# Attention scores of two groups at once in four PSUM banks, with 64-row matmuls for the low part of g, maxima read from PSUM and three output banks in turn

## The chip, the cores and the metric

The kernel runs on one core of one Trainium2 chip. The metric is the time of one execution on the device, in microseconds (us). A core has a matrix engine (TensorE, PE in the profile; its weight loads are PEld), VectorE (DVE), ScalarE (ACT), GpSimd (POOL) and SyncE (SP), whose queue issues the transfers here. They run side by side and wait for one another by semaphores. Matmul results land in PSUM, eight banks of 128 partitions x 512 f32; all else is in SBUF.

## The reference

A group norm, then self-attention over the 4096 pixels of each of four images of 256 channels, then two residual additions:

```python
x: (4, 256, 64, 64) float32;  C = 256, CQ = 64, N = 4096
xg = group_norm(x, G=32, eps=1e-5)           # per image
xf = xg.reshape(4, 256, 4096)
f = Wq @ xf;  g = Wk @ xf;  h = Wv @ xf      # 64, 64 and 256 rows
scores = f.T @ g                             # n x m, 4096 x 4096
beta = softmax(scores, axis=n)               # over n, for each column m
out = x + gamma * (h @ beta) + xf
```

## The kernel before, in words

Each f32 operand of a matmul is split into an f16 high and an f16 low part. The products kept are high x high, high x low and low x high.

An image (a batch) is cut into 16 column blocks of M = 256 columns m; there are K = 64 blocks. The 4096 rows n of a block are 32 tiles of 128, in G = 8 groups of GT = 4 tiles. A group of scores is thus 4 tiles x 256 columns, 1024 f32 on each partition, two banks.

`scores(q)` (L346, matmuls L354 and L355) computes group q = 8k + g into `S`. The stationary operand is a tile of `F1`, with the high part of f on partitions 0 to 63 and its low part on 64 to 127. `G1` holds the high part of g on both halves, `GL` the low part on both halves. Two matmuls of 128 rows and 256 columns per tile give (fh + fl) x (gh + gl). ScalarE's `store` (L451) copies `S` into `SC` in SBUF. VectorE's `maximum` (L586, the first a copy L579, the last into `MX` by L584) folds `SC` into the running maximum `XM`, in PSUM, in halves of 512 columns. `quadrant_maxima` (L591, L593, L600), a tiny f32 matmul `share_maxima` (L376), `column_maxima` (L608) and `spread_maxima` (L615) turn this into a row `MB` of column maxima. `subtract` (L621) takes it off the stored scores, `exps` (L457, L458) on ScalarE makes the exponentials, once rounded to f16 (`PH`) and once f32, and GpSimd's `low_weights` (L277) makes the low part `PL`. `weigh(n)` (L368 to L370) multiplies a group by V, 24 matmuls of 256 or 257 columns (the extra column of ones gives the softmax's denominator), accumulating in two banks of `O`, the pair of banks `k % 2`. `divide` (L640) and `scale_output` (L647) then finish the block, `turn_blocks` (L655) turns it in 32 x 32 blocks, 16 small transfers regroup these (`regroup` on SP), and GpSimd adds the residual.

The order of each engine is written out by hand. The main loop goes over n = 8k + g. TensorE computes the scores of group n + 16, two blocks ahead, and then weighs group n. VectorE subtracts for group n + 4, ScalarE makes the exponentials of n + 3, GpSimd the low weights of n + 3. The rings of `PH` and `PL` have 4 places, so exponentials of n + 3 wait until group n - 1 is weighed. SP, once per block, regroups and stores the block before and loads the residual input of the next.

Work for the next image is mixed in: in blocks j = 1 to 4 of an image (at g = 5) statistics, in block 5 the variances (`group_variances`, L529 to L544), in block 6 the roots (`inverse_roots`, L550 to L564), in blocks 7 to 10 normalising (L568) and splitting of x. In blocks 13 and 14 stand the f/g projections, `project_fg` (eight units of 512 columns, 6 matmuls each, L329 to L331; the evacuation is `round_fg` L463 to L465 and `low_fg` L627 to L629), in block 15 and block 0 of the next image the V projections, `project_v` (eight units of 4 tiles, 24 matmuls each, L341 to L343; `round_v` L471, `low_v` L635). They use the pair of `O` banks of the other parity. Before the loop, a head does all this for the first image, and the scores of blocks 0 and 1.

PSUM: `O` four banks, `S` two, `XM` one, `MB` one.

## Time and profile before

| what | us |
|---|---|
| median of 3 runs | 2033.85 (2032.63 to 2034.09) |
| the profiled execution | 2034.04 |
| its span, first to last instruction | 2032.3 |
| TensorE busy, matmuls | 1954.7 |
| VectorE busy | 1712.7 |
| ScalarE busy | 1611.6 |
| GpSimd busy | 1313.2 |

The span runs from the first to the last instruction; the time of an execution has a little more around it. Busy times of matmuls are modelled from their starts, and a matmul's duration is longer than the distance to the next one's start, since they are pipelined; so starts are to be compared, not durations. A row of the timeline gives the start, the duration, the engine, the line, the operation and its operands, and in brackets how long the engine was idle before it and who released it.

### The profile page before, as it was taken

The numbers are of one execution on the slowest core, as the hardware profiler recorded it, in microseconds if no ns is written. First come the engines' busy times: TensorE is split into PE (matmuls) and PEld (weight loads), VectorE is DVE, ScalarE is ACT, GpSimd is POOL, SyncE is SP. The second block draws the span as 40 slices with busy tenths as digits, with TensorE's granted clock in tenths as the row PEclk, the third lists the DMA queues.
The fourth block names the chain that finished last, engine by engine and source line by source line (L and its number), as shares of the span: only waits on it lengthen the run. The fifth ranks groups of instructions, "written<-read, shape, count | busy, mean of one in ns | idle before, by whom it ended". The sixth has DMA issues, their size and how long they took to land.

```text
span 2032.3 us, 43482 instructions
## 1 busy us (share of the span) xinstructions
PE 1954.7 (96%) x17476; PEld 1698.7 (84%) x17476; DVE 1712.7 (84%) x2469; ACT 1611.6 (79%) x1699; POOL 1313.2 (65%) x746
## 2 busy tenths in 40 slices
PE   3899999999999999999999999999999999999999
PEld 1688888888788888888778888888878888888887
DVE  8798899988868899998886989999787778887784
ACT  4588878888767887988876888788887788888885
POOL 3066668886546666887544676688645566667667
PEclk9899999999999999999999999999999999999999
DMA  2012211211002221221110221121111011111111
GB/s 96 1 32 72 71 31 43 73 30 30 19 20 69 55 62 27 66 61 22 27 22 23 67 71 51 22 73 51 30 22 27 17 32 22 32 30 30 32 22 43
DMA packets 188746, 82.68 MB, mean 41 GB/s; under 512 B 148352, under 2 KB 181376, under 8 KB 188544
## 3 DMA queue, kind: packets, MB, share of 16 engines
q1 hardware_dynamic: 188544, 79.90, 14.8%
q8 instruction: 137, 2.24, 0.5%
q14 instruction: 65, 0.53, 0.1%
HBM read 46.53 MB, written 16.78 MB: 31 GB/s over the span
## 4 chain that ended last, share of the span: by engine, by line
PE 87%; DVE 9%; issue 2%; ACT 1%; DMA 1%; SPq 0%; DVEq 0%; ACTq 0%
PE O L369 20%; PE O L370 20%; PE O L368 20%; PE S L354 10%; PE S L355 10%; DVE XM L586 2%; DVE SC L621 2%; PE O L341 1%; PE O L343 1%; PE O L342 1%; PE O L329 1%; PE O L331 1%; PE O L330 1%; DMA SC<-x 1%; DVE gt L556 1%
## 5 line engine op out<-in xcount | busy, mean ns | idle before, releaser
L277 POOL TENSOR_TENSOR PL<-SC,PH 128x1024 f16<-128x1024 f32 x512 | 1091.9, 2135 | 683.9 <-ACT SC L458 679.6
L369 PE MATMUL O<-V,PH 128*128 128x256 f16 x4096 | 1119.9, 273 | 0.0
L368 PE MATMUL O<-V,PH 128*128 128x257 f16 x4096 | 1116.4, 273 | 2.0 <-DVE GL L629 2.0
L370 PE MATMUL O<-V,PL 128*128 128x257 f16 x4096 | 1113.4, 272 | 0.0
L451 ACT ACTIVATE SC<-S 128x1024 f32<-128x1024 f32 x512 | 524.3, 1024 | 275.4 <-PE S L355 273.1
L586 DVE TENSOR_TENSOR XM<-SC,XM 128x512 f32<-128x512 f32 x896 | 616.2, 688 | 134.2 <-ACT SC L451 119.6
L621 DVE TENSOR_TENSOR SC<-SC,MB 128x1024 f32<-128x1024 f32 x512 | 618.8, 1209 | 0.7
L457 ACT ACTIVATE PH<-SC 128x1024 f16<-128x1024 f32 x512 | 537.6, 1050 | 27.5 <-DVE SC L621 19.4
L458 ACT ACTIVATE SC<-SC 128x1024 f32<-128x1024 f32 x512 | 536.1, 1047 | 0.0
L354 PE MATMUL S<-G,F 128*128 128x256 f16 x2048 | 479.0, 274 | 18.2 <-ACT SC L451 13.6
L355 PE MATMUL S<-GL,F 128*128 128x256 f16 x2048 | 479.1, 274 | 0.0
L370 PEld LDWEIGHTS O<-V,PL 128*128 128x128 f16 x4096 | 402.4, 98 | 52.6
L368 PEld LDWEIGHTS O<-V,PH 128*128 128x128 f16 x4096 | 394.3, 96 | 61.3 <-issue 2.8
L369 PEld LDWEIGHTS O<-V,PH 128*128 128x128 f16 x4096 | 396.1, 97 | 56.5 <-issue 0.3
L354 PEld LDWEIGHTS S<-G,F 128*128 128x128 f16 x2048 | 206.4, 101 | 47.5 <-ACT SC L451 11.2
L355 PEld LDWEIGHTS S<-GL,F 128*128 128x128 f16 x2048 | 201.3, 98 | 23.9 <-issue 0.3
L635 DVE TENSOR_TENSOR V<-O,V 128x1024 f16<-128x1024 f32 x32 | 39.2, 1225 | 78.4 <-ACT V L471 78.4
L296 POOL TENSOR_TENSOR RES<-RES,ATT 128x512 f32<-128x512 f32 x63 | 81.8, 1299 | 1.5 <-DMA ATT<-OT 1.5
L471 ACT CAST V<-O 128x1024 f16<-128x1024 f32 x32 | 32.4, 1012 | 60.6 <-PE O L343 60.6
L341 PE MATMUL O<-wvh,XH 128*128 128x256 f16 x256 | 70.6, 276 | 9.9 <-issue 6.8
L286 POOL TENSOR_SCALAR RES<-xres,rscale,rbias 128x256 f32<-128x256 f32 x128 | 78.7, 624 | 0.0
L342 PE MATMUL O<-wvl,XH 128*128 128x256 f16 x256 | 70.5, 275 | 0.0
(81 smaller groups left out, 1000.8 us busy)
## 6 DMA issues: line engine op xcount, KB each, us to landing
xin<-x SPq DMA_DIRECT2D x24, 1024.0 KB, 5.7
xres<-x SPq DMA_DIRECT2D x64, 256.0 KB, 2.9
out<-RES SPq DMA_DIRECT2D x64, 256.0 KB, 2.2
ATT<-OT SPq DMA_DIRECT2D x1008, 16.0 KB, 1.9
SC<-x SPq DMA_DIRECT2D x4, 1024.0 KB, 8.4
wv<-wvT SPq DMA_DIRECT2D x1, 256.0 KB, 10.3
wqk<-wqT SPq DMA_DIRECT2D x1, 64.0 KB, 10.5
wqk<-wkT SPq DMA_DIRECT2D x1, 64.0 KB, 10.5
```

The source lines that it names most:

```text
L277: pool.tensor_tensor(PL[:, s % RING, :], sc(s), PH[:, s % RING, :], ALU.subtract).then_inc(pl_ready, 1)
L341: mm(o, xh, wvh[:, h, :], start=h == 0, stop=False)
L354: mm(S[:, i * M:(i + 1) * M], f, G1[:, cols], start=True, stop=False)
L355: m = mm(S[:, i * M:(i + 1) * M], f, GL[:, cols], start=False, stop=True)
L368: mm(o[:, 0:C + 1], PH[:, n % RING, cols], vh, start=t == 0, stop=False)
L369: mm(o[:, 0:C], PH[:, n % RING, cols], vl, start=False, stop=False)
L370: w = mm(o[:, 0:C + 1], PL[:, n % RING, cols], vh, start=False, stop=t == T - 1)
L451: nc.scalar.activation(sc(q), S[:, :], ACT.Copy).then_inc(s_stored, 1)
L457: nc.scalar.activation(PH[:, s % RING, :], sc(s), ACT.Exp, bias=SHIFT)
L458: nc.scalar.activation(sc(s), sc(s), ACT.Exp, bias=SHIFT).then_inc(exp_done, 1)
L586: ve.tensor_tensor(XM[:, :], part, XM[:, :], ALU.max).then_inc(s_maxed, 1)
L621: ve.tensor_tensor(tile, tile, MB[:, 0:M].unsqueeze(1).to_broadcast([P, GT, M]), ALU.subtract).then_inc(sub_ready, 1)
```

## The change

**Scores.** `S` has four banks, two for an even group and two for the odd one after it. `scores(q)` runs at even g only and computes groups q and q + 1. For each group the high part of g is multiplied as before, by matmuls of 128 rows (4 per group). The low part is multiplied by the high part of f alone, in matmuls of 64 rows: `F1` now has the high part of f on partitions 0 to 63 for even units of 512 columns and on 64 to 127 for odd ones, so that of a pair of groups one uses the upper and the other the lower half of the array. Order: four full, eight half (alternating between the groups), four full.

**Maxima.** VectorE takes a group's maximum straight from `S` in one operation of 1024 columns, with `XM` now in SBUF. The first group of a block has none of its own: the second is compared with the stored copy of the first. VectorE takes the odd group while ScalarE stores the even one, then they change places. Once per block `fold_maxima` reduces 1024 to 256 columns. TensorE waits for both maxima and both stores before the next scores.

**Output banks.** `O` has three banks: block k uses banks 2k and 2k + 1 modulo 3, the third (`spare`) serves the shared maxima and the projections. `weigh` runs by bank, 12 matmuls for the first and 12 for the second. V projections are units of two tiles, 16 per image, in the middle (`MID`) or at the end (`END`) of a group.

**Doubling g.** ScalarE and VectorE write g's parts once; a transfer per unit on SP (`double_g`) copies both parts to the other half. The weights Wq are loaded a second time, so that odd units come out of the projection with the halves changed. Weights and V have another place or stride.

The core of the diff:

```diff
+        GG = sb("GG", [P, 2, N], f16)
+        G1, GL = GG[:, 0, :], GG[:, 1, :]
+        XM = sb("XM", [P, GW], f32)
-        O = ctx.enter_context(nc.psum_tensor("O", [P, 2, MB2, 512], f32))
-        S = ctx.enter_context(nc.psum_tensor("S", [P, GW], f32))
-        XM = ctx.enter_context(nc.psum_tensor("XM", [P, 512], f32))
+        O = ctx.enter_context(nc.psum_tensor("O", [P, OB, 512], f32))
+        S = ctx.enter_context(nc.psum_tensor("S", [P, 2, GW], f32))
...
+            def double_g(u):
+                f, g = halves(u)
+                n = slice(u % NFG * FGW, (u % NFG + 1) * FGW)
+                sp.wait_ge(fg_done, u + 1)
+                sp.dma_start(GG[f, :, n], GG[g, :, n]).then_inc(g_in[u % NFG], 16)
...
             def scores(q):
-                if q > 0:
-                    pe.wait_ge(s_stored, q)
-                for i in range(GT):
-                    f = F1[:, (g * GT + i) * P:(g * GT + i + 1) * P]
-                    mm(S[:, i * M:(i + 1) * M], f, G1[:, cols], start=True, stop=False)
-                    m = mm(S[:, i * M:(i + 1) * M], f, GL[:, cols], start=False, stop=True)
-                m.then_inc(s_ready, 1)
+                for a in range(2):
+                    if q > 0:
+                        pe.wait_ge(s_maxed, q)
+                        pe.wait_ge(s_stored, q - 1 + a)
+                    for i in (0, 2):
+                        mm(to(a, i), F1[:, rows(a, i)], G1[:, cols], start=True, stop=False)
+                for i in (0, 2, 1, 3):
+                    for a, half in enumerate((slice(0, CQ), slice(CQ, P))):
+                        mm(to(a, i), F1[half, rows(a, i)], GL[half, cols], start=i % 2 == 1, stop=i % 2 == 0)
+                for a in range(2):
+                    for i in (1, 3):
+                        m = mm(to(a, i), F1[:, rows(a, i)], G1[:, cols], start=False, stop=True)
+                    m.then_inc(s_ready, 1)
...
+                if g % 2 == 0 and k + 2 < K:
...
                     scores(n + 2 * G)
+                pe.wait_ge(pl_ready, n + 1)
...
+                weigh(n, 0)
+                extra(k, g, MID)
+                if g == 2 and k + 1 < K:
...
+                    share_maxima(k + 1, spare(k))
+                if g == 0 and k > 0:
+                    pe.wait_ge(osb_ready, MB2 * (k - 1) + 1)
+                weigh(n, 1)
+                extra(k, g, END)
...
             def store(q):
                 act.wait_ge(s_ready, q + 1)
+                if q % 2 == 1:
+                    act.wait_ge(s_maxed, q)
...
+            for s in range(EXP_LEAD):
+                exps(s)
             for n in range(K * G):
                 if n + EXP_LEAD < K * G:
                     exps(n + EXP_LEAD)
+                if g % 2 == 0 and k + 2 < K:
+                    store(n + 2 * G)
+                    store(n + 2 * G + 1)
...
+            def fold_maxima(c):
+                dve.wait_ge(s_maxed, G * (c + 1))
...
+                ve.tensor_reduce(MX[:, :], XM[:, :].rearrange("p (i m) -> p m i", i=GT), axis=AX.X,
+                                 op=ALU.max).then_inc(mx_ready, 1)
+            def maximum(q):
+                c, g = divmod(q, G)
+                scores = S[:, q % 2, :]
+                dve.wait_ge(s_ready, q + 1)
+                if g == 0:
+                    return
+                if g == 1:
+                    dve.wait_ge(s_stored, q)
...
+                    ve.tensor_tensor(XM[:, :], scores, sc(q - 1), ALU.max).then_inc(s_maxed, 2)
+                    return
+                if q % 2 == 0:
+                    dve.wait_ge(s_stored, q + 1)
+                dve.wait_ge(s_maxed, q + 1 if q % 2 == 0 else q - 1)
+                ve.tensor_tensor(XM[:, :], scores, XM[:, :], ALU.max).then_inc(s_maxed, 1)
...
+            for s in range(SUB_LEAD):
+                subtract(s)
             for n in range(K * G):
                 if g == 0 and k > 0:
                     divide(k - 1)
+                    scale_output(k - 1)
+                if g % 2 == 0 and k + 2 < K:
+                    maximum(n + 2 * G + 1)
                 if n + SUB_LEAD < K * G:
                     subtract(n + SUB_LEAD)
+                if g % 2 == 0 and k + 2 < K:
+                    maximum(n + 2 * G)
+                if g == 7 and k + 2 < K:
+                    fold_maxima(k + 2)
```

## Rows read from the trace of the kernel before

**Rows 1.** The page: busy time by engine, and the granted clock by slice (tenths).

```profile
PE 1954.7 (96%) x17476; PEld 1698.7 (84%) x17476; DVE 1712.7 (84%) x2469; ACT 1611.6 (79%) x1699; POOL 1313.2 (65%) x746
...
PEclk9899999999999999999999999999999999999999
```

**Rows 2.** The page: the chain that ended last, by engine.

```profile
PE 87%; DVE 9%; issue 2%; ACT 1%; DMA 1%; SPq 0%; DVEq 0%; ACTq 0%
```

**Rows 3.** Timeline of VectorE, the reciprocals: start us, us, engine, line, operation, idle before.

```profile
242.55 0.17 DVE L640 RECIPROCAL rden<-O 128x2 f32<-128x2 f32 x1 [0.89 <-PE O L370]
...
360.07 0.16 DVE L640 RECIPROCAL rden<-O 128x2 f32<-128x2 f32 x1
...
473.02 0.17 DVE L640 RECIPROCAL rden<-O 128x2 f32<-128x2 f32 x1 [0.89 <-PE O L370]
...
626.27 0.17 DVE L640 RECIPROCAL rden<-O 128x2 f32<-128x2 f32 x1 [0.76 <-PE O L370]
...
1701.59 0.17 DVE L640 RECIPROCAL rden<-O 128x2 f32<-128x2 f32 x1 [0.89 <-PE O L370]
...
1729.88 0.17 DVE L640 RECIPROCAL rden<-O 128x2 f32<-128x2 f32 x1 [0.89 <-PE O L370]
```

**Rows 4.** Timeline of TensorE, last V matmuls, scores, first weighing (98 to 101.3 us).

```profile
98.05 0.27 PE L341 MATMUL O<-wvh,XH 128*128 128x256 f16 x1
...
100.34 0.27 PE L354 MATMUL S<-G,F 128*128 128x256 f16 x1
...
101.21 0.27 PE L368 MATMUL O<-V,PH 128*128 128x257 f16 x1
```

**Rows 5.** Timeline of ScalarE in a plain block (1727 us).

```profile
1727.23 1.03 ACT L451 ACTIVATE SC<-S 128x1024 f32<-128x1024 f32 x1 [0.60 <-PE S L355]
1728.15 1.05 ACT L457 ACTIVATE PH<-SC 128x1024 f16<-128x1024 f32 x1
```

**Rows 6.** The waits: who waited for whom, us, times, longest.

```profile
ACT SC L451 <- PE S L355: 273.1, 420, 2.1
```

**Rows 7.** Timeline of VectorE in a plain block (1705 us).

```profile
1705.08 1.21 DVE L621 TENSOR_TENSOR SC<-SC,MB 128x1024 f32<-128x1024 f32 x1
1706.21 0.69 DVE L586 TENSOR_TENSOR XM<-SC,XM 128x512 f32<-128x512 f32 x1
1706.81 0.70 DVE L591 STREAM_TRANSPOSE MT<-MX 128x512 f32<-128x512 f32 x1
```

**Rows 8.** Timeline of TensorE's loads and matmuls after a wait (1007.4 us).

```profile
1007.40 0.10 PEld L368 LDWEIGHTS O<-V,PH 128*128 128x128 f16 x1 [0.92 <-issue]
1007.44 0.27 PE L368 MATMUL O<-V,PH 128*128 128x257 f16 x1 [0.67 <-DVE GL L629]
```

**Rows 9.** Timeline of TensorE around the f32 matmuls of the maxima (1711.9 us).

```profile
1711.94 0.31 PE L376 MATMUL O<-mxs,alike 128*128 128x32 f32 x2
1712.08 0.27 PE L354 MATMUL S<-G,F 128*128 128x256 f16 x1
```

**Rows 10.** Groups of instructions by line and form: busy us, mean ns, idle before.

```profile
L635 DVE TENSOR_TENSOR V<-O,V 128x1024 f16<-128x1024 f32 x32 | 39.2, 1225 | 78.4 <-ACT V L471 78.4
...
L471 ACT CAST V<-O 128x1024 f16<-128x1024 f32 x32 | 32.4, 1012 | 60.6 <-PE O L343 60.6
...
L376 PEld LDWEIGHTS O<-mxs,alike 128*128 128x128 f32 x128 | 19.3, 191 | 5.7 <-DVE mxs L600 5.0
```

**Rows 11.** Timeline of VectorE: variances, roots and the maximum after each, a normalising.

```profile
261.03 0.60 DVE L529 BATCH_NORM_AGGREGATE mv<-stats 128x2 f32<-128x48 f32 x2
...
269.86 0.70 DVE L586 TENSOR_TENSOR XM<-SC,XM 128x512 f32<-128x512 f32 x1
...
293.29 0.22 DVE L550 TENSOR_SCALAR gt<-gvar 128x4 int32<-128x4 int32 x1
...
300.98 0.69 DVE L586 TENSOR_TENSOR XM<-SC,XM 128x512 f32<-128x512 f32 x1
...
324.40 3.35 DVE L568 TENSOR_SCALAR xin<-xin,nmean,nrstd 128x1024 f32<-128x1024 f32 x2
```

More of the change, by code:

```diff
@@ L142, in groupnorm_attention @@
         fg_done = sem("fg_done")
+        g_in = [sem(f"g_in{i}") for i in range(NFG)]
         v_ready = sem("v_ready")
@@ L252, in _ @@
                         load(b + 1, p)
+                    for place, i in FG_AT.items():
+                        if place[0] == j:
+                            double_g((b + 1) * NFG + i)
             store(K - 1)
```

378 lines of the change are left out of this document (198 added, 180 removed).

## Prediction, made before the changed kernel ran

> **What bounds the kernel now.** I read the page first. TensorE is busy 96% of the span, at the full clock in nearly every slice [rows 1], and 87% of the chain that ended last lies on it [rows 2]. So the time is nearly the sum of what TensorE issues. Next I took the timeline and looked for the period of the loop: the reciprocal L640 runs once per column block, so two of them in a row bound a block. A plain block takes 1729.88 - 1701.59 = 28.29 us [rows 3]. On TensorE, 21 matmuls of 256 columns start between 98.05 and 100.34, so one start follows the other after 0.109 us [rows 4]; I call this a slot. A duration of 0.27 us is the way of one matmul through the array, not its price. A block has 8 groups of 24 weighing and 8 score matmuls, 256 slots, and 256 x 0.109 = 27.9 us, so a plain block is TensorE without holes. In it ScalarE waits 0.60 us for TensorE's scores in each group of 28.29/8 = 3.54 us, so it works at most 2.94 us of it [rows 5]; over the run that wait is 273 us [rows 6]. VectorE spends 1.13 us on a subtraction and 0.60 us on half a maximum [rows 7].
>
> Where is TensorE not the limit? In blocks 5 to 8 of a batch, where VectorE has the group-norm arithmetic of the next batch to do: 360.07 - 242.55 = 117.52 us against 4 x 28.29 = 113.2, a loss of 4.4 us. And in blocks 13 to 15 and the next block 0, where the projections of the next batch are mixed in: 626.27 - 473.02 = 153.25 us against 113.2 + 20.9 for 192 V matmuls of a slot each + 10.5 for 48 f/g matmuls of 512 columns, two slots each: 8.7 us lost [rows 3]. Each happens three times.
>
> The profiled execution took 2034.04 us, its span 2032.3. The 1.7 us outside it stay. The median is 2033.85, so no correction is needed between the two.
>
> **The score matmuls (the gain).** Two groups cost 16 slots now, 1.744 us. After, they are 8 full matmuls and 8 of 64 rows. Two of the latter sit in different halves of the array and write different banks; if they run side by side, four slots hold the eight, and a pair costs 12 x 0.109 = 1.308 us. The main loop computes the scores of 62 blocks, 248 pairs, so each 0.1 us on a pair is 24.8 us. The full gain is 0.436 x 248 = 108.1 us.
>
> The trace of before has no matmul of 64 rows, so two prices are unknown. The first is the change between full and half array, twice a pair. Below, I take nothing: the f32 matmuls of L376 stand between f16 ones without a hole. Above, I take that the array must run empty first: 0.27 - 0.11 = 0.16 us of way left after a slot, and 0.04 us from a load to its matmul where TensorE came out of a wait (1007.40 and 1007.44), 0.20 us in all [rows 4, 8]. It cannot be below nothing, since no matmul is saved by it. The nearest row is L376: its two matmuls of 32 columns take 1712.08 - 1711.94 = 0.14 us, 0.07 each with its weight load, where 32 of 256 columns would be a few hundredths [rows 9]. Some 0.05 us over the columns is what an unlike matmul costs there, and I take 0.05 us per change, 0.10 per pair.
>
> The second is the rate of loads. Each half matmul has a load of its own; side by side, a load and a matmul must start every 0.055 us. The densest that the trace shows is again 0.07 us, for f32 weights, whose load takes 0.19 us against 0.10 for f16 [rows 8, 10]. I take 0.055 as reached, since an f16 load is half as long, and 0.07 as the other end.
>
> So a pair costs 1.308 + 0.10 = 1.408 us, and 0.336 x 248 = **83.3 us** go.
>
> The Trainium skill, "TensorEngine Tiling (Array Packing)", section Tiling Modes, Key Properties, says that changing the tiling mode drains TensorE, which speaks against this change. It gives no duration. By the row's bound the drains would take nearly the whole gain, and the time is the one of the third rival below.
>
> **The maxima and who waits for them.** Before, VectorE reads scores from SBUF after ScalarE stored them; TensorE waits for ScalarE only (`s_stored`). After, VectorE reads PSUM itself, and TensorE's next pair waits for both maxima (`s_maxed`). Behind that wait stands everything of TensorE. Load: before, a block has 8 subtractions and 16 half maxima, 8 x 1.13 + 16 x 0.60 = 18.6 us; after, 8 subtractions, 7 maxima and one fold, each of 1024 columns. The subtraction L621 also has one operand in PSUM and 1024 columns, so I price all at 1.13: 16 x 1.13 = 18.1 us, and the transpose and reduction after the fold halve to 256 columns [rows 7]. VectorE is not busier, but the block shrinks by 4 x 0.336 = 1.3 us.
>
> Does the handshake fit? Let a pair start on TensorE at 0; it lasts 48 x 0.109 + 1.41 = 6.6 us. Scores are ready at 1.5. VectorE: odd maximum to 2.6, subtraction to 3.8, even maximum to 4.9. ScalarE: two exponentials of at most 1.05 us from 0.2 to 2.3, even store (0.92) to 3.2, odd store to 4.1 [rows 5]. The next pair needs both at 6.6. At a block's start the divide and scale delay the odd maximum by about 1 us, but that pair has no even one. Cost in plain blocks: nothing; the cover is 1.7 us. ScalarE's work on a pair is at most 5.9 us, 0.7 less than the period, so it does not become the bound either.
>
> It does not fit where VectorE has a long uninterruptible run in group 5. Computing the variances takes 269.86 - 261.03 = 8.83 us and the roots 300.98 - 293.29 = 7.69 us [rows 11]. From the start of the pair of group 4: even maximum done 4.9, subtraction 6.05, variances 14.9, then odd maximum, subtraction, even maximum 18.3. TensorE wants to start the next block's scores at 13.3, so it stands 5.0 us; for the roots 3.9 us. Together 8.9 us per batch against the 4.4 lost now, so 4.5 x 3 = **13.5 us** are given back. Normalising (3.35 us in block 7, where 6.05 + 3.35 + 3.4 = 12.8) is just covered.
>
> **Projections, queues, head.** An f/g unit has two roundings and two low parts, not three; the third goes to a DMA on SP's queue, which waits there for `fg_done` behind the block's regroup and store and ahead of the next block's. Those are due later than the projections, and the doubled g is read a block or more later: nothing. But one spare bank now serves all projections, so each unit waits for the one before to be emptied; the order leaves some 1.3 us of weighing between two V units, and emptying 512 columns (a rounding, then a low part) takes about as long: half of 1012 and of 1225 ns, 1.1 us, and the signals [rows 10]. I book no difference to the 8.7 us lost per batch now, with 4 us per batch either way. The number of V and projection matmuls is the same. Splitting `weigh` by bank changes the order alone; the wait of its second half for `osb_ready` comes 2.6 us into a block, VectorE's scale is done at about 1.9: nothing. The new stride of V changes no count: nothing.
>
> In the head, f/g work on VectorE and ScalarE shrinks by a third, but the first subtractions and exponentials are no longer mixed into the V units: after the last V unit come rounding, low part, subtraction, two exponentials and the low weights, some 6 us, with only 1.4 us of scores over them. Now weighing begins at 101.21, right behind the scores [rows 4]. I take 3 us more, between -8 and +8.
>
> **The sum.** 2034.0 - 83.3 + 13.5 + 3 = 1967.2, so 1967 us.
>
> **The rivals.** *Free changes.* Changing array mode costs nothing: 2034 - 108.1 + 16.5 = 1942 us; were the VectorE stalls hidden too, 1926. For it: TensorE takes unlike matmuls without a hole. Against: L376's 0.07 us. *Loads set the half phase.* Eight halves at 0.07 us are 0.56, not 0.436 us: a pair costs 1.532, 0.212 x 248 = 52.6 us gained, 2034 - 52.6 + 16.5 = 1998 us. *Slower than before: the array empties at each change.* 0.40 us per pair, all but 0.036 x 248 = 8.9 us of the gain gone, while the new VectorE stalls and the head still cost 16.5: 2034 - 8.9 + 16.5 = 2042 us. The change turns slower when the two switches cost over 0.436 - 16.5/248 = 0.37 us a pair, 0.19 each. For it: no row shows matmuls of both array modes in flight together; against: none shows any emptying either. *The change does not do what it says:* the halves run one after the other, a slot each: 1.744 + 0.10 us a pair, 2034 + 24.8 + 16.5 = 2075 us. For it: each of them needs its own load.
>
> **How the numbers follow.** Forecast as summed, 0.45; free changes 0.23; loads 0.13; emptying 0.14; one after the other 0.05. The forecast's own range is 1950 to 1990. The range 1934 to 2043 cuts off the part of free changes with hidden stalls (0.08) and the upper half of the slow cases (0.11). A measurement of this kernel tells about 0.2% from no change, 4 us. Faster: the first three cases and a rest of the emptying, 0.82. Within 0.2%: 0.03, all from emptying that costs about 0.19 us a change. Slower: 0.15.
>
> **What would show it.** In the timeline of TensorE: half matmuls that start in pairs close together and four pairs in 0.44 us; the hole at the two changes, 0.05 us forecast; a plain block of 28.29 - 1.34 = 26.9 us between reciprocals. In the waits: TensorE's scores waiting for VectorE's maximum some 4 to 5 us in blocks 5 and 6 of each batch, and hardly elsewhere. ScalarE's wait for scores should fall to well under half of 273 us. The prediction is wrong if plain blocks have waits of TensorE on maxima (the handshake is tighter than worked out), if a maximum from PSUM costs clearly over 1.13 us, or if the pair of scores lies outside 1.31 to 1.71 us.

## The result, and the profile after

| what | before | after |
|---|---|---|
| median of 4 runs each, us | 2033.91 | 2014.78 (2013.05 to 2015.34) |
| span of the profiled execution, us | 2032.3 | 2013.6 |
| TensorE busy, matmuls, us | 1954.7 | 1915.7 |
| VectorE busy, us | 1712.7 | 1661.2 |
| ScalarE busy, us | 1611.6 | 1591.8 |

The changed kernel takes 0.9908 of the time of before (95% interval 0.9896 to 0.9921): 19 us faster, where 67 were forecast. Each ratio here and below is taken against executions of the kernel before in the same series (medians from 2032.35 to 2033.91), and each difference in us is against 2014.78 unless said. The lines of its page that answer [rows 1]:

```profile
PE 1915.7 (95%) x17476; PEld 1567.4 (78%) x17476; DVE 1661.2 (83%) x2021; ACT 1591.8 (79%) x1699; POOL 1312.0 (65%) x746
PEclk9899999999999998999999999999999999999999
```

I read the plain block first, against [rows 3]: the timeline of VectorE after, the reciprocals (now L741).

```profile
1693.08 0.23 DVE L741 RECIPROCAL rden<-O 128x1 f32<-128x1 f32 x2
...
1720.39 0.24 DVE L741 RECIPROCAL rden<-O 128x1 f32<-128x1 f32 x2
...
1747.69 0.22 DVE L741 RECIPROCAL rden<-O 128x1 f32<-128x1 f32 x2
```

A plain block takes 27.30 us, 0.99 less than the 28.29 of before, where 1.34 were forecast. Times 62 that is 61 us. Now the pair of scores in such a block, in the timeline of TensorE after (a row with x4 or x8 is so many instructions in a row, from the first start to the last end):

```profile
1732.77 0.60 PE L400 MATMUL S<-GG,F 128*128 128x256 f16 x4
1733.31 0.61 PE L403 MATMUL S<-GG,F 64*128 64x256 f16 x8
1733.85 0.61 PE L406 MATMUL S<-GG,F 128*128 128x256 f16 x4
1734.30 0.27 PE L418 MATMUL O<-V,PH 128*128 128x257 f16 x1
```

The pair lasts 1734.30 - 1732.77 = 1.53 us. Eight half matmuls end 0.61 us after the first starts; in single slots they would need 7 x 0.109 + 0.27 = 1.03. So they run two at a time, eight in the time of four. The view of stretches, for this line alone, gives the number under way (PE, in the first brackets) in two stretches of 0.02 us:

```profile
1733.38:1733.40 0.02, 0.02 (x2) 0.02 (x4) 1.00 0.00 0
1733.42:1733.44 0.02, 0.02 (x4) 0.01 (x2) 1.00 0.00 0
```

They come in pairs, one pair after the other at the distance of a slot. From the first of them to the next full matmul pass 0.54 us, four slots and 0.10; from the first full one to the first half, again 0.54, four slots and 0.10. So each change of the array's mode costs about 0.10 us, where 0.05 was taken. The first half matmul starts at 1733.31, while the four full ones end at 1732.77 + 0.60 = 1733.37: by these modelled ends the array is not empty at the change.

Then the blocks with the next image's arithmetic. Blocks 5 to 10 of the first image take 31.68, 32.81, 29.53, 28.07, 28.05 and 28.06 us, 14.4 us over six plain blocks; before, 4.4 were lost there. The two stalls of TensorE in its timeline after:

```profile
273.93 0.60 PE L400 MATMUL S<-GG,F 128*128 128x256 f16 x4 [2.85 <-issue]
...
306.69 1.04 PE L400 MATMUL S<-GG,F 128*128 128x256 f16 x4 [3.67 <-DVE XM L677]
```

Four matmuls behind the second stall take 1.04 us instead of 0.60. The view of stretches shows why; the third column from the end is the granted clock. After, from the first stall on:

```profile
273.90:276.75 2.85, 2.82 (x21) 1.87 (x22) 2.85 (x2) 2.59 (x3) 1.94 (x1) 0.69 0.01 3
276.75:303.00 26.25, 26.25 (x239) 21.85 (x237) 23.00 (x36) 18.77 (x20) 17.39 (x11) 0.97 0.14 31
306.69:309.56 2.87, 2.87 (x17) 1.55 (x18) 2.87 (x2) 2.61 (x3) 1.94 (x1) 0.50 0.00 0
309.56:316.00 6.44, 6.44 (x47) 5.17 (x46) 6.23 (x12) 4.18 (x5) 2.40 (x3) 0.77 0.01 3
316.00:339.00 23.00, 23.00 (x221) 19.15 (x219) 19.33 (x18) 19.62 (x21) 18.88 (x11) 1.00 0.16 35
```

and before, block 5 with the variances and block 6 with the roots:

```profile
242.55:275.52 32.97, 32.61 (x298) 28.63 (x297) 31.28 (x47) 25.51 (x28) 21.09 (x12) 1.00 0.18 54
275.52:306.64 31.12, 28.74 (x260) 24.95 (x259) 30.03 (x51) 23.35 (x26) 19.38 (x12) 1.00 0.11 27
```

After each of the two stalls TensorE works for a few us at its lower level of 1.2 GHz (0.50 right behind the second); before, it stays at the full clock in these two blocks. The part of the clock that is missing is worth 0.31 x 2.85 + 0.03 x 26.25 + 0.50 x 2.87 + 0.23 x 6.44 = 4.6 us per batch. Not all of that would come back at the full clock, as the kernel with the halves in a row shows below.

In blocks 8 to 10 nothing of that kind is left, yet each takes 0.76 us more than a plain block. The timeline of VectorE after, around the normalising in block 8:

```profile
385.52 3.35 DVE L650 TENSOR_SCALAR xin<-xin,nmean,nrstd 128x1024 f32<-128x1024 f32 x2
388.79 1.21 DVE L677 TENSOR_TENSOR XM<-S,XM 128x1024 f32<-128x1024 f32 x1
389.92 1.21 DVE L713 TENSOR_TENSOR SC<-SC,MB 128x1024 f32<-128x1024 f32 x1
391.05 1.21 DVE L677 TENSOR_TENSOR XM<-S,XM 128x1024 f32<-128x1024 f32 x1
392.18 1.21 DVE L713 TENSOR_TENSOR SC<-SC,MB 128x1024 f32<-128x1024 f32 x1
393.31 1.98 DVE L656 TENSOR_REDUCE MX<-XM 128x256 f32<-128x1024 f32 x1
395.21 0.21 DVE L741 RECIPROCAL rden<-O 128x1 f32<-128x1 f32 x2
395.46 1.00 DVE L749 TENSOR_SCALAR OSB<-O,rden,gam 128x256 f32<-128x256 f32 x2
```

and what TensorE then waits for:

```profile
396.06 0.28 PE L418 MATMUL O<-V,PH 128*128 128x257 f16 x1 [0.21 <-DVE OSB L749]
```

VectorE comes out of the 3.35 us with no pause up to the reciprocal, so `divide` and `scale_output` of the block before are late, and TensorE waits for the bank that they empty. Start to start, this costs 0.38 us over a slot, half of the 0.76. The rest stands further on in the block, in the pair of scores and at `share_maxima`:

```profile
400.02 0.72 PE L400 MATMUL S<-GG,F 128*128 128x256 f16 x4
403.15 0.38 PE L427 MATMUL O<-mxs,alike 128*128 128x32 f32 x2
```

The second group's full matmuls come 0.13 us late, behind ScalarE's store, which ends at 400.22; `share_maxima` costs some 0.25 us more than in a plain block, behind VectorE's `mxs`, which ends at 403.01. The fold of the maxima is in VectorE's row of work too, and it takes 1.98 us where 1.13 were priced.

Head: the first reciprocal is at 135.76 instead of 129.41. The first weighing in the timeline of TensorE after, against the last row of [rows 4]:

```profile
106.29 0.40 PE L418 MATMUL O<-V,PH 128*128 128x257 f16 x1 [5.25 <-POOL PL L312]
```

It waits 5.25 us for the first low weights, starts 5.1 us later than before, and behind that wait, from 106.29 to 109.40, the granted clock is 0.50. Blocks 13 to 15 and the next block 0 take 150.07 us against 109.2 for four plain ones and 31.4 for the matmuls of the projections: 9.5 us lost per batch; before, 8.7 in the first batch and 7.0 in the other two. That difference of 1.6 us before is the clock too: TensorE stands 2.28 us in block 14 of the first batch and 2.29 in that of the second, but only behind the first, in the 6 us from 523.70, is the granted clock 0.72; behind the second it is 1.00. So the 8.7 us that the prediction took for each of three batches hold for one.

So from the reciprocals of all 64 blocks the difference comes together: 6.35 us at the first reciprocal, -60.1 for 61 blocks of scores behind it at 0.985, +29.5 for blocks 5 to 10 of three batches, +5.8 for the projections, -0.4 for the last two blocks, which compute no scores: -18.9. The last reciprocal is at 2008.14 instead of 2026.91, 18.8 earlier.

The waits after, of ScalarE and of TensorE for the maximum (us in total, times, longest), against [rows 6]:

```profile
ACT SC L524 <- issue: 133.2, 82, 5.2
ACT PH L530 <- PE O L420: 119.3, 233, 0.8
...
ACT SC L524 <- PE S L406: 7.4, 7, 2.9
...
PE S L400 <- DVE XM L677: 14.8, 5, 3.7
```

ScalarE's wait for scores is 7 us by name, but it has moved rather than gone: 133 us stand before the store with another cause, 119 before the exponentials, for a free place in the ring of `PH`.

### The profile page after: what moved, and what is told of

Same layout as the page of the kernel before. It is cut to its first block and busy times, and to the rows that moved or that the text cites. A ratio compares the mean times of both kernels' runs of the same rounds, so it can differ in the third digit from the quotient of the medians.

```text
span 2013.6 us, 44173 instructions
## 1 busy us (share of the span) xinstructions
PE 1915.7 (95%) x17476; PEld 1567.4 (78%) x17476; DVE 1661.2 (83%) x2021; ACT 1591.8 (79%) x1699; POOL 1312.0 (65%) x746
## 3 DMA queue, kind: packets, MB, share of 16 engines
q8 instruction: 139, 2.28, 0.5%
## 5 line engine op out<-in xcount | busy, mean ns | idle before, releaser
L524 ACT ACTIVATE SC<-S 128x1024 f32<-128x1024 f32 x512 | 502.6, 1013 | 150.4 <-issue 133.2
L677 DVE TENSOR_TENSOR XM<-S,XM 128x1024 f32<-128x1024 f32 x384 | 468.2, 1219 | 151.6 <-PE S L406 149.7
L400 PE MATMUL S<-GG,F 128*128 128x256 f16 x1024 | 157.6, 275 | 26.5 <-DVE XM L677 14.8
L406 PE MATMUL S<-GG,F 128*128 128x256 f16 x1024 | 160.2, 280 | 0.0
L403 PE MATMUL S<-GG,F 64*128 64x256 f16 x2048 | 159.6, 276 | 0.0
L400 PEld LDWEIGHTS S<-GG,F 128*128 128x128 f16 x1024 | 99.1, 98 | 47.7 <-issue 20.6
L406 PEld LDWEIGHTS S<-GG,F 128*128 128x128 f16 x1024 | 80.3, 99 | 62.5 <-issue 55.6
L403 PEld LDWEIGHTS S<-GG,F 64*128 64x128 f16 x2048 | 80.0, 95 | 61.6 <-issue 54.9
L656 DVE TENSOR_REDUCE MX<-XM 128x256 f32<-128x1024 f32 x64 | 125.6, 1962 | 0.1
L672 DVE TENSOR_TENSOR XM<-S,SC 128x1024 f32<-128x1024 f32 x64 | 78.4, 1225 | 53.8 <-ACT SC L524 52.6
L727 DVE TENSOR_TENSOR V<-O,V 128x512 f16<-128x512 f32 x64 | 43.7, 689 | 73.3 <-ACT V L544 73.3
L544 ACT CAST V<-O 128x512 f16<-128x512 f32 x64 | 37.1, 587 | 76.1 <-PE O L379 76.1
```

The costliest lines, as they stand in the source:

```text
L400: mm(to(a, i), F1[:, rows(a, i)], G1[:, cols], start=True, stop=False)
L403: mm(to(a, i), F1[half, rows(a, i)], GL[half, cols], start=i % 2 == 1, stop=i % 2 == 0)
L406: m = mm(to(a, i), F1[:, rows(a, i)], G1[:, cols], start=False, stop=True)
L524: nc.scalar.activation(sc(q), S[:, q % 2, :], ACT.Copy).then_inc(s_stored, 1)
L677: ve.tensor_tensor(XM[:, :], scores, XM[:, :], ALU.max).then_inc(s_maxed, 1)
```

## The experiments

Three things had to be told apart: what the scores' part is worth and what a change of mode costs; what the next image's arithmetic costs and by which mechanism; and whether the rest (head, fold, normalising) is what it seems. All diffs are against the changed kernel unless said.

**The low part of g on the full array.**

```diff
-    mm(to(a, i), F1[half, rows(a, i)], GL[half, cols], start=i % 2 == 1, stop=i % 2 == 0)
+    mm(to(a, i), F1[:, rows(a, i)], GL[:, cols], start=i % 2 == 1, stop=i % 2 == 0)
```

> The changed kernel, with the low part of g multiplied on the whole array (128 rows) as before, all else kept: no change of array mode, 16 slots per pair. Theory A, side by side works and each change of mode costs 0.10 us: a pair costs 1.744 us where the changed kernel's trace has 1.53, so a plain block takes 4 x 0.21 = 0.86 us more than 27.30, 28.15, and the run 248 x 0.21 = 53 us more, less what the longer blocks give VectorE back: 2055 to 2068 us, slower than the kernel before; the rest of the change then costs 20 to 35 us by itself. Rival B, the matmuls of 64 rows bring little and the gain comes from the maxima and the three banks: within 10 us of 2015.

Measured 2054.39 us, 1.0108 of before (1.0093 to 1.0123), 0.6 us under the range expected. Plain blocks take 28.20 us, 0.90 more than after, 0.225 a pair (0.436 for four slots less two changes: 0.105 each). So the 64-row matmuls are worth 40 us, and everything else in the change costs 22 us against before (2032.47 in this series).

**Four changes of mode instead of two.** Two full matmuls stand before and two behind the part shown.

```diff
+                for i in (0, 1):
+                    for a, half in enumerate((slice(0, CQ), slice(CQ, P))):
+                        mm(to(a, i), F1[half, rows(a, i)], GL[half, cols], start=i % 2 == 1, stop=i % 2 == 0)
+                for a in range(2):
+                    mm(to(a, 1), F1[:, rows(a, 1)], G1[:, cols], start=False, stop=True)
+                    mm(to(a, 2), F1[:, rows(a, 2)], G1[:, cols], start=True, stop=False)
+                for i in (2, 3):
+                    for a, half in enumerate((slice(0, CQ), slice(CQ, P))):
+                        mm(to(a, i), F1[half, rows(a, i)], GL[half, cols], start=i % 2 == 1, stop=i % 2 == 0)
```

> The changed kernel with its score matmuls in another order: two full, four half, four full, four half, two full, so four changes of array mode per pair for two, the same matmuls. Theory A, a change costs 0.10 us wherever it stands: 0.21 us more per pair, plain block 27.30 + 0.84 = 28.1, run 2014.8 + 50 = 2065 us. Rival B, the 0.2 us of holes in a pair are the pace of the half matmuls' loads or a price of the phase as a whole: nothing or less than 10 us more.

Measured 2055.19 us (1.0111, 1.0096 to 1.0126), 10 us under the expectation. Plain blocks take 28.14 us, 0.84 more, so 0.21 a pair and 0.105 us for each added change. Between the last start before and the first after a change the timeline has 0.09 to 0.10 us beyond a slot. The total rose by 40 and not by 62 x 0.84 = 52 us, since the blocks that wait for VectorE absorb a part (blocks 5 to 10 of the first image take 178.96 us here and 178.20 in the changed kernel). The two experiments give the same price by opposite routes: one takes two changes away, the other adds two. The Trainium skill, "TensorEngine Tiling (Array Packing)", Key Properties, says that a change drains TensorE. The trace agrees that a change costs time, but the 0.105 us is half of the 0.20 that [rows 4, 8] set as the price of an array that must run empty, and the half matmuls start before the modelled end of the full ones.

**The halves in a row.** All four halves of the upper group, then all four of the lower.

```diff
-    for i in (0, 2, 1, 3):
-        for a, half in enumerate((slice(0, CQ), slice(CQ, P))):
+    for a, half in enumerate((slice(0, CQ), slice(CQ, P))):
+        for i in (0, 2, 1, 3):
```

> The changed kernel with the eight 64-row matmuls in another order: the four of the upper half of the array, then the four of the lower, not alternating. Theory A, matmuls start in the order of the program and only neighbours in different halves run together: each but one takes a slot of its own, 3 x 0.109 to 4 x 0.109 us more per pair, a plain block 27.3 + 1.3 to 1.74 = 28.6 to 29.0 us, run 2014.8 + 80 to 105 = 2095 to 2120 us. Rival B, TensorE pulls the lower half's matmuls ahead: within 10 us of 2015.

Measured 2013.70 us (0.9904, 0.9891 to 0.9918), as after. The timeline of TensorE in this kernel:

```profile
1737.31 0.60 PE L400 MATMUL S<-GG,F 128*128 128x256 f16 x4
1737.85 0.62 PE L403 MATMUL S<-GG,F 64*128 64x256 f16 x8
1738.40 0.61 PE L406 MATMUL S<-GG,F 128*128 128x256 f16 x4
```

Eight halves again end in 0.62 us, and again two at a time. The first four in the program use one half of the array only, so if two run together because they sit in different halves, the lower four run beside upper ones that stand ahead of them in the program. My expectation that the order matters fell. Which half a record belongs to the trace does not tell, and a rival is left: a 64-row matmul might take half a slot wherever it sits. No run had all eight in one half. The Trainium skill, "TensorE: Matmul & The Clock Gate", Part 3 (what overlaps and what doesn't), has matmuls start strictly in program order; by that rule, with the slots of these rows, the lower four would start behind three slots of the upper, and I estimate 6 x 0.109 + 0.27 = 0.92 us for the eight. This run, with 0.62, speaks against it for matmuls in different rows of the array, unless the rival holds.

This kernel also shows what the lower clock is worth. In each of its three batches TensorE stands 3.67 us in block 6, and the granted clock behind it differs (third column from the end):

```profile
305.83:312.70 6.87, 6.87 (x42) 4.65 (x43) 6.74 (x9) 4.78 (x5) 4.27 (x2) 0.61 0.01 2
797.86:804.73 6.87, 6.87 (x50) 5.16 (x51) 6.74 (x9) 5.05 (x6) 4.26 (x2) 0.75 0.01 2
1289.13:1296.00 6.87, 6.15 (x57) 4.92 (x58) 6.76 (x9) 5.05 (x6) 4.28 (x2) 1.00 0.00 0
```

Block 7 takes 29.33, 28.51 and 27.72 us in them. So a stall of that length need not be followed by the lower clock, and the lowest of these clocks costs 1.6 us against the full one, though 0.39 x 6.87 = 2.7 us of clock are missing: at the full clock TensorE soon waits 0.72 us (at 1292.88) for VectorE's late scale.

**No variances and roots of the next image**, in the changed kernel and in the kernel before.

```diff
-                        group_variances(b + 1)
+                        pass
...
-                        inverse_roots(b + 1)
+                        ve.tensor_scalar(rscale[:, (b + 1) % 2, :], nrstd[:, 0:H], 1.0, None, ALU.add)
+                        ve.scalar_tensor_tensor(rbias[:, (b + 1) % 2, :], nmean[:, 0:H], -1.0, nrstd[:, 0:H],
+                                                ALU.mult, ALU.mult).then_inc(res_coefs, 1)
```

> The changed kernel without the variances and roots of images 1 to 3: they are normalised with the coefficients of image 0. Theory A, VectorE's long runs in blocks 5 and 6 hold back the maxima, so the scores, and the pause then lowers TensorE's clock, 9 to 10 us of stalls and slow matmuls net per image in blocks 5 to 7: 2015 - 25 to 30 = 1985 to 1990 us, with granted clock 1.00 in those blocks. Rival B, TensorE's lost time there is due to normalising and transfers: less than 8 us gained.

> The kernel before with the same part left out, the variances and roots of images 1 to 3. There a block 5 to 8 of an image loses 4.4 us in all and TensorE waits for ScalarE's stores alone. Theory A: 3 x 4.4 = 13 us gained, 2021 us, half of what the same edit gives the changed kernel, so the rest is the new wait and the clock. Rival B, the runs cost both kernels the same: the same 25 to 30 us, 2006 us.

Measured 1981.26 us (0.9745, 0.9729 to 0.9761), 33.5 less than after, 11.2 per batch and more than the 25 to 30 expected; and 2018.96 us (0.9933, 0.9918 to 0.9948), 13.5 less than before (2032.47 in this series), 4.5 per batch. In the first, blocks 5 and 6 take 27.26 and 27.24 us, in the timeline of VectorE:

```profile
244.73 0.23 DVE L741 RECIPROCAL rden<-O 128x1 f32<-128x1 f32 x2
...
271.99 0.23 DVE L741 RECIPROCAL rden<-O 128x1 f32<-128x1 f32 x2
...
299.23 0.22 DVE L741 RECIPROCAL rden<-O 128x1 f32<-128x1 f32 x2
```

and blocks 7 to 10 take 28.34 and three times 28.06: 3.3 us over plain blocks, which is the normalising alone. So the 14.4 lost per batch are 11.2 for this arithmetic (2.85 + 3.67 = 6.5 of stalls and 4.7 behind them, where the stretches gave 4.6 for the missing clock) and 3.3 for the normalising. Before, the whole loss of 4.4 was this arithmetic, and normalising was all but free (block 7 keeps 0.2 us).

**The same arithmetic in pieces.** First ten pieces, one at each of the groups 2 to 6 of blocks 5 and 6; then twelve smaller ones, the last two in groups 2 and 3 of block 7. A piece has one to five small operations; in the second kernel the steps of the roots' iteration come two at a time. The diff is that of the first.

```diff
-                    if j == VARS_AT:
...
-                        group_variances(b + 1)
-                    if j == ROOTS_AT:
-                        inverse_roots(b + 1)
...
+                if 2 <= g <= 6 and b + 1 < BATCH and j in (VARS_AT, ROOTS_AT):
+                    some_coefs(g, variance_steps if j == VARS_AT else root_steps, b + 1)
```

> The changed kernel with the same arithmetic for the variances and roots, cut into five pieces per block that stand at groups 2 to 6 of blocks 5 and 6 instead of one run at group 5. Theory A, it is the length of the run that holds back the maxima and then the clock: most of the 33.5 us that leaving the work out gave come back, 20 to 30 us, 1985 to 1995 us, blocks 5 and 6 at 28 us and clock 1.00 throughout. Rival B, VectorE has too much to do in these blocks whatever its order: under 12 us gained.

Measured 1998.34 us (0.9830, 0.9815 to 0.9844), 16.4 less: short of the expectation. TensorE still stalls for 2.06 us in block 6 (3.01 in the second batch). The cause is in the timeline of VectorE in this kernel, three operations on 4 numbers per partition:

```profile
293.03 1.50 DVE L642 SCALAR_TENSOR_TENSOR gt<-gr 128x4 f32<-128x4 f32 x1
294.56 1.20 DVE L643 TENSOR_TENSOR gt<-gt,gvar 128x4 f32<-128x4 f32 x1
295.79 2.05 DVE L644 SCALAR_TENSOR_TENSOR gr<-gt,gr 128x4 f32<-128x4 f32 x1
```

and of GpSimd:

```profile
292.38 2.13 POOL L312 TENSOR_TENSOR PL<-SC,PH 128x1024 f16<-128x1024 f32 x1 [1.20 <-ACT SC L531]
294.47 1.27 POOL L331 TENSOR_TENSOR RES<-RES,ATT 128x512 f32<-128x512 f32 x1
295.70 2.12 POOL L312 TENSOR_TENSOR PL<-SC,PH 128x1024 f16<-128x1024 f32 x1
```

Each of the three ends within 0.03 us of a GpSimd instruction (294.53 and 294.51, 295.76 and 295.74, 297.84 and 297.82); with GpSimd idle (from 291.2 to 292.4) the same operations take 0.16 us. The Trainium skill, "SBUF — State Buffer", Who interferes with whom, says that a VectorE instruction with two inputs in SBUF, or a copy or scalar operation in a two-port mode, and a GpSimd instruction that reads SBUF keep each other out for a whole instruction. The trace agrees, and it is why 8.83 and 7.69 us of [rows 11] are so long for so little data: before, L541 on 32 numbers per partition takes 2.12 us and ends at 266.33, beside low weights of GpSimd that end at 266.28.

> The changed kernel with the arithmetic of the coefficients in twelve pieces of at most two or three operations, at groups 2 to 6 of blocks 5 and 6 and groups 2 and 3 of block 7. In the run with ten pieces one piece of three operations took 4.75 us, as each waited for GpSimd, and TensorE stood 2.06 us behind it and then had a clock of 0.94. Theory A, only the length of the longest run counts: no stall over 1 us, clock 1.00, another 5 to 8 us gained on the ten pieces' 1998.3: 1990 to 1994 us. Rival B, the sum of VectorE's work in these blocks is the bound by now: within 3 us of 1998.

Measured 1989.93 us (0.9788, 0.9774 to 0.9801), 24.9 less, as expected. The stretches of blocks 5 to 7 in this kernel:

```profile
243.27:270.90 27.63, 27.63 (x264) 23.28 (x262) 26.53 (x39) 23.72 (x25) 19.65 (x12) 1.00 0.16 42
270.90:299.66 28.76, 28.53 (x270) 23.78 (x267) 27.84 (x40) 23.69 (x25) 19.39 (x12) 1.00 0.12 29
299.66:328.90 29.24, 27.48 (x258) 22.82 (x258) 28.82 (x35) 23.82 (x26) 21.16 (x12) 1.00 0.12 28
```

The clock stays full, with no stall over 1.10 us left. In the kernel with ten pieces the stall of 2.06 us was followed by a clock of 0.84 over the 11 us behind it in the first batch, and by 1.00 over 11 us in the third. So with the same operations in shorter runs the stalls go and the lower clock with them; the two gains are not told apart by this run.

**The small values in PSUM**, so that fewer operations have all of their operands in SBUF.

```diff
-        cm = sb("cm", [P, 32], f32)
-        cv = sb("cv", [P, 32], f32)
...
-        gmean = sb("gmean", [P, NG], f32)
...
-        gt = sb("gt", [P, NG], f32)
...
+        cm, cv = MB[:, 288:320], MB[:, 320:352]
...
+        gmean, gsum, gt = MB[:, 384:388], MB[:, 388:392], MB[:, 392:396]
```

> The changed kernel with the same arithmetic in one run at group 5, but the small intermediate values (means, squares, the roots' helper) in free columns of a PSUM bank, so that nearly each operation has one operand there. Theory A, an operation of VectorE whose operands are all in SBUF waits for the end of GpSimd's running instruction, one with an operand in PSUM does not: operations of 1.2 to 2.1 us fall to 0.2, the runs of 8.8 and 7.6 us to 3 to 4.5 us, stalls and low clock in blocks 5 to 7 mostly go, 22 to 30 us gained, 1985 to 1993 us. Rival B, they wait for something else (a semaphore, SBUF's ports in general): the runs keep over 7 us and the time stays within 4 us of 2014.8.

Measured 1995.92 us (0.9820, 0.9804 to 0.9836), 18.9 less, short of the 22 to 30 expected. The run of the variances shrinks from 6.75 to 3.1 us, that of the roots only from 7.63 to 6.9. The timeline of VectorE in this kernel (`gr` is in SBUF, `MB` here holds `gt`, in PSUM):

```profile
290.65 2.02 DVE L636 SCALAR_TENSOR_TENSOR MB<-gr 128x4 f32<-128x4 f32 x1
292.70 0.17 DVE L637 TENSOR_TENSOR MB<-MB,gvar 128x4 f32<-128x4 f32 x1
292.90 0.16 DVE L638 SCALAR_TENSOR_TENSOR gr<-MB,gr 128x4 f32<-128x4 f32 x1
293.10 0.80 DVE L636 SCALAR_TENSOR_TENSOR MB<-gr 128x4 f32<-128x4 f32 x1
```

GpSimd runs without a pause from 290.51 to 295.96. L637 and L638, with one input in PSUM and one in SBUF, do not wait; L636, which reads `gr` twice, does, though its result goes to PSUM. So it is the inputs that decide for an operation with two of them. A stall of 2.90 us stays in block 6.

**The normalising in halves**, one half in group 3 and one in group 5.

```diff
-                        for h in range(H):
-                            last = normalise(xin[:, h, :], h)
+                if g in (3, 5) and b + 1 < BATCH and NORM_FIRST <= j < NORM_FIRST + NPC:
+                    h = (g - 3) // 2
...
+                    last = normalise(xin[:, h, :], h)
```

> The changed kernel with its normalising in two halves, one at group 3 and one at group 5 of blocks 7 to 10, not both at group 5. Those blocks take 28.06 us where plain ones take 27.30, with TensorE waiting for VectorE's scale at the start of the next. Theory A, VectorE comes late only since the 3.4 us follow each other behind its last free time: 12 blocks x 0.76 = 9 us at most, 2006 to 2010 us. Rival B, VectorE is full in these blocks: within 2 us of 2014.8.

Measured 2019.55 us (0.9933, 0.9919 to 0.9946), 4.8 slower than after: a miss. The groups by form, this kernel and after:

```profile
L650 DVE TENSOR_SCALAR xin<-xin,nmean,nrstd 128x1024 f32<-128x1024 f32 x24 | 62.4, 2599 | 0.0
```

```profile
L650 DVE TENSOR_SCALAR xin<-xin,nmean,nrstd 128x1024 f32<-128x1024 f32 x24 | 40.2, 1715 | 0.0
```

Each half meets a GpSimd instruction of its own and waits for it (one starts at 329.00, beside low weights that run from 328.93 to 331.06, and ends at 331.62, 0.56 us behind them); two halves in a row wait once. Blocks 8 to 10 take 28.85 us in place of 28.06, 7 us in all; in the profiled execution a part of it is won back in blocks 6 and 7 of the second batch, where no lower clock follows the first stall, and in the head. Cutting work on VectorE into pieces helps only where a piece does not pay for a wait of its own.

**The fold by a transposition**: 1024 columns are transposed in 32 x 32 blocks and reduced in one operation with the maxima's second step.

```diff
-                ve.tensor_reduce(MX[:, :], XM[:, :].rearrange("p (i m) -> p m i", i=GT), axis=AX.X,
-                                 op=ALU.max).then_inc(mx_ready, 1)
+                ve.transpose(MT[:, :], XM[:, :]).then_inc(mx_ready, 1)
...
-                ve.transpose(MT[:, :], MX[:, :]).then_inc(mx_turned, 1)
+                ve.tensor_reduce(mxq, MT[:, :].rearrange("p (i j n) -> p j i n", i=GT, j=NB), axis=AX.XY,
+                                 op=ALU.max).then_inc(mx_turned, 1)
...
```

> The changed kernel with the fold of the maxima done otherwise: XM is transposed whole (1024 columns) and one reduction goes over groups of 32 and over the four tiles, in place of the strided reduction (1.96 us), a transpose (0.40) and a reduction (0.43). 2.4 us for 2.8. Theory A, in normalising blocks VectorE comes late to the scale at a block's start and TensorE waits 0.22 us, and in blocks 5 and 6 each us of VectorE counts: 3 to 6 us gained, 2009 to 2012 us. Rival B, the fold's cost is covered everywhere: within 1 us of 2014.8.

Measured 2018.33 us (0.9928, 0.9913 to 0.9942), 3.5 slower: a miss. The transposition takes 1237 ns and the reduction 1190 in place of 1962, 404 and 428, so 0.37 us less in all. The part before the reciprocal shrinks by 0.73 us, but the part between the scale and the shared maxima grows by 0.36, and in the normalising block at 371 to 375 us TensorE now waits 0.36 us for a store and 0.33 for `mxs`, where the changed kernel's rows show no idle time. Less work on VectorE, at a less favourable place. Blocks 8 to 15 and the next block 0 take 2.5 us more per batch; in the profiled execution a part of these 7.5 us is won back in the head and behind stalls without the lower clock.

**The first subtractions and exponentials between the V units of the head**, as in the kernel before.

```diff
-            for s in range(EXP_LEAD):
-                exps(s)
+                if 11 <= u < 11 + EXP_LEAD:
+                    exps(u - 11)
...
-            for s in range(SUB_LEAD):
-                subtract(s)
...
+                if u >= 10 and u < 10 + SUB_LEAD:
+                    subtract(u - 10)
```

> The changed kernel with the first four subtractions and three exponentials placed among the last V units of the head, as in the kernel before, not behind them. Theory A, they are the pause of 5.25 us before the first weighing, and the half clock from 106.3 to 111.1 follows from it: 5.25 + 2.4 = 7.6 us gained at most, some of it lost to longer waits of the V units: 2008 to 2010 us. Rival B, the V units' handshake is the bound there and they grow by what the pause shrinks: under 2 us.

Measured 2008.91 us (0.9884, 0.9869 to 0.9899), 5.9 less, as expected. The first weighing starts at 102.69 instead of 106.29, the first reciprocal is at 129.79. So the head's loss is the missing overlap, as the prediction said, with the clock behind the wait, and larger than it said. The head itself varies: its first reciprocal lies between 133.96 and 135.76 in the five kernels that share it unchanged, and at 129.41 and 127.70 in the two with the head of before, so its loss is known to within some 2 us.

**Together.** Three kernels combine them: ten pieces, turned fold and early exponentials; then twelve pieces, halves of the normalising and early exponentials; then twelve pieces and early exponentials alone.

> The three edits together: coefficients in pieces, turned fold, early exponentials. If their causes are separate their gains add: 25 + 4 + 6 us, 1980 us. If the fold only mattered while VectorE was late in blocks 5 and 6, the sum falls short by 2 to 4 us.

> The changed kernel with twelve pieces, normalising in halves and the early exponentials of the head. If the three causes are separate: 2014.8 - 23 - 7 - 6 = 1979 us, between 1974 and 1986. If VectorE is full in blocks 5 to 10, it stays at 1988 or more.

> The changed kernel with the coefficients in twelve pieces and the early exponentials of the head, normalising left whole. If the two losses are separate, their gains of 24.9 and 5.9 us add: 1984 us, between 1982 and 1986. If the head's gain is only shifted (the first blocks then wait), 1988 or more.

Measured 1995.95 us (0.9819, 0.9802 to 0.9835), 1994.68 us (0.9811, 0.9798 to 0.9825) and 1984.47 us (0.9762, 0.9747 to 0.9776). The first two missed by 16 us. In the first the fold took back 3.5 us again (1998.3 - 5.9 = 1992.4 without it) and the ten pieces had fallen short before; in the second the halves cost 10.2 us against the third, which differs in them alone, more than by themselves. The third is as expected: 24.9 + 5.9 = 30.8 us less were to be had, 30.3 came.

> The same with the small values in PSUM as well. In twelve pieces blocks 5 to 7 still took 85.6 us for 81.9, with waits of 1.1 us for VectorE's scale. Theory A: with pieces of 0.6 us for up to 4 these go, 3 x 3 us: 1975 to 1978 us. Rival B, VectorE's whole load in blocks 5 to 7 is the bound: within 2 us of the run before it.

The last adds the values in PSUM: 1980.90 us (0.9744, 0.9730 to 0.9759), 3.6 less where 6 to 9 were expected. Blocks 5 to 7 take 27.63, 27.36 and 29.40 us. It beats both kernels: 51 us less than before (2032.35 in this series), 34 less than the change. In it TensorE computes the same matmuls as after.

## Why the prediction was right and wrong

Two steps failed. The term for the change of array mode, 0.05 us, was mis-sized: it measured 0.105 us and took 22 us of the gain. And the 13.5 us given back in the blocks with the next image's arithmetic came as 29.5: the lower clock behind a stall was put at nothing without a reason, and normalising, called "just covered", was not. The pace of the half matmuls and the handshake in plain blocks were right.

- *The bound and the slot* were right: TensorE's starts, 0.109 us apart, make up the plain block before and after.
- *Side by side* was right as to the time, eight loads and matmuls in four slots, two at a time. The rival that loads set the half phase wanted 0.56 us and a change for the eight; first half to next full matmul is 0.54 with the change. The rival of one after the other wanted 0.87 and a change.
- *The change of mode* was mis-sized: 0.105 us, not 0.05. I had taken the row of the small f32 matmuls [rows 9] as the nearest; the value lies about midway between nothing and the upper bound of 0.20 worked out from [rows 4, 8]. The loads show where the time goes: elsewhere the next load starts with the matmul before it, but at a change it starts 0.20 us behind the start of the last matmul (1733.30 against 1733.10) and right with its own. So a pair saves 0.246 us by the plain blocks (0.225 by the kernel with full low parts), not 0.336, and 22 us of the forecast gain did not come. The break-even of 0.19 was not reached, which is why the sign held.
- *The handshake in plain blocks* was right: no stall of TensorE on a maximum there, a plain block is again TensorE without holes but for the changes. A maximum from PSUM takes 1219 ns, as a subtraction.
- *The stalls of blocks 5 and 6* were forecast as 5.0 and 3.9 us and came as 2.85 and 3.67; the run of the variances was 6.75 us this time, not 8.83, as it met other GpSimd instructions. By itself this term was too pessimistic, by 2.4 us a batch.
- *The clock behind a stall* was missing. I priced a pause of TensorE at its own length. It cost 4.7 us a batch more, 14 us in all, by the stretches. As a single cause it is worth less, since at the full clock a part would have become waiting: 1.6 us behind the second stall, by the three batches of the kernel with the halves in a row. No run kept both stalls at the full clock throughout.
- *Normalising "just covered"* failed: 3.3 us a batch, 10 us in all. I had followed the maxima to the next scores and found cover, and had not followed VectorE's queue further, to `mxs` and above all to the reciprocal and the scale that free an output bank, which I had put down as ready at 1.9 us into a block in every case. The fold, priced at 1.13 and 1.96 us long, stands in that queue.
- *Projections*: 0.8 us more in the first batch and 2.5 to 2.7 in the others, within the 4 us either way, 5.8 in all; no run tells the cause. The 8.7 us that were taken as lost before in each batch hold for the first one, the others lost 7.0.
- *Head*: 3 us forecast, between -8 and +8; 7.3 came (6.35 at the first reciprocal and the 0.99 that block 0 had saved by then), of which the early exponentials give back 5.9. The missing overlap was named, its size was not, and the lower clock behind the wait of 5.25 us was left out here as well.
- *The sum.* The result lies 48 us above the forecast of 1967: 22 for the changes of mode, 16 for blocks 5 to 10 (29.5 against 13.5: clock +14, normalising +10, stalls -7, and 1 less by rounding and the slightly shorter blocks of the other two batches), 6 for the projections, 4 for the head.
- Of the rivals none was the result. *Free changes*, *loads*, *emptying* and *one after the other* all turned on the pair of scores alone; over half of the error lay elsewhere, where I had no rival at all. The 1998 us of *loads* come nearest, by luck: their reason did not hold. The 1926 us of free changes with hidden stalls also drop the 3 us of the head, without saying so.

What stays open: why a change costs 0.105 us, about a slot, why the load behind it starts late, and whether this depends on the number of columns; no run here varied that. Whether two 64-row matmuls in the same half would also share a slot was not tried. That the late scale is half of the loss of the normalising blocks was read from the timeline; no run moved the reciprocal ahead of the fold. When a stall of 2 to 4 us is followed by the lower clock and when not, no run here decides.

## What to carry over

When work moves to a bounding engine's new partner, follow that partner's queue to every release it makes, not only to the one that the change adds, and price a stall of TensorE with a chance of the lower clock behind it, less the waiting that the lower clock covers. Before cutting a long run of small VectorE operations into pieces, look which of them have their inputs in SBUF while GpSimd works: those wait for it, and each piece may pay anew. A gain that depends on an unseen price of the array needs one small experiment, since here the price was a slot per change and took half the gain.

## What the runs showed of the hardware

- A change between 128-row and 64-row matmuls costs 0.105 us on TensorE (256 columns, f16, full clock), measured with two more changes and with two fewer.
- Four pairs of 64-row matmuls in different halves of the array take the time of four full ones, loads included (eight in 0.61 and 0.62 us from first start to last end), whether they alternate or stand in two rows of four in the program.
- Pauses of TensorE and the granted clock behind them: 1.10 us, 1.00; 2.06 us, 0.84 over 11 us; 2.85 us, 0.69 over 2.85 us; 3.67 us, 0.50 over 2.87 us. But also: 2.06 us, 1.00 over 11 us (ten pieces, third batch); 2.68 us, 1.00 over 11 us (the first kernel of the three together, first batch); 3.67 us, 1.00 over 6.87 us (halves in a row, third batch).
- VectorE's operations on 4 elements take 0.16 us, and up to 2.05 us when both inputs are in SBUF and GpSimd is running; with one of the two in PSUM they took 0.16 to 0.17 us.
- A reduction of 1024 elements whose innermost step is 256 elements (to 256 results) takes 1.96 us, one over neighbours (to 8 results) 1.19 us.
